# A two-layer kernel on one core: four reorderings around a saturated TensorE

## The reference, cut to what matters

```
# layer 0, x is (4, 512, 512) float32, V = 512, H = 2048
q, k, v = x @ Wq, x @ Wk, x @ Wv
attn_out = softmax(q k^T * V**-0.5) @ v @ Wp + bp
cms_out  = gelu(attn_out @ cW1 + cb1) @ cW2 + cb2 + one_hot(codes)
modifier = gelu(concat[attn_out, cms_out] @ mW1 + mb1) @ mW2 + mb2
x = clip(x + cms_out + modifier, 0, 1)
# layer 1, the adapter: weights picked by stream
h = gelu(x @ W_down[stream] + b_down[stream]) @ W_up[stream] + b_up[stream]
out = layernorm(x + h) * ln_w[stream] + ln_b[stream]
```

## Time and profile before

| | |
|---|---|
| time, median of 3 runs | 1076.12 us (1076.08 to 1076.13) |
| profiled execution's own time | 1076.47 us |
| its span | 1074.7 us |
| PE busy | 1064.8 us, 99% of the span |
| PEld, DVE, POOL, ACT busy | 882.2, 595.4, 541.8, 455.7 us |

### The profile page before, as it was taken

The page is one execution under the profiler, slowest core; times in us unless marked ns, Lnnn a source line. Parts: engine busy times, 40 slices in busy tenths (PEclk is TensorE's granted clock), DMA queues, the critical chain, the costliest instruction groups (busy, mean ns, idle before and its releaser), DMA issues.

```text
span 1074.7 us, 13175 instructions
## 1 busy us (share of the span) xinstructions
PE 1064.8 (99%) x4756; PEld 882.2 (82%) x4756; DVE 595.4 (55%) x837; ACT 455.7 (42%) x871; POOL 541.8 (50%) x555
## 2 busy tenths in 40 slices
PE   9999999999999999999999999999999999999997
PEld 8888888888888888888878888888878888888886
DVE  3735344395565565565764445445885454545568
ACT  4624336353343343333454333343644433342675
POOL 0501154542243232332798667666997667753415
PEclk9999999999999999999999999999999999999999
DMA  7401010101223213102222222224935221124863
GB/s 275 138 1 40 1 40 20 40 0 45 74 73 127 95 73 105 39 34 65 71 96 84 84 84 66 82 84 146 355 108 171 84 79 57 62 69 148 293 118 118
DMA packets 62064, 100.51 MB, mean 94 GB/s; under 512 B 5680, under 2 KB 35376, under 8 KB 61488
## 3 DMA queue, kind: packets, MB, share of 16 engines
q1 hardware_dynamic: 61424, 98.62, 27.1%
q10 hardware_dynamic: 576, 1.05, 0.3%
HBM read 77.63 MB, written 22.02 MB: 93 GB/s over the span
## 4 chain that ended last, share of the span: by engine, by line
PE 90%; DVE 4%; POOL 4%; ACT 1%; issue 1%; DMA 0%; ACTq 0%; DVEq 0%; POOLq 0%
PE bank L735 29%; PE bank L736 29%; PE bank L737 29%; DVE z L1512 1%; POOL left_c L567 1%; DVE stats L1506 1%; PE bank L789 1%; DVE c_T_f L1311 1%; POOL c_B_lo L567 1%; POOL rawC L581 1%; POOL W_lo L567 0%; DVE acc L1388 0%; PE bank L761 0%; POOL left_x L567 0%; POOL c_T_lo L567 0%
## 5 line engine op out<-in xcount | busy, mean ns | idle before, releaser
L1388 DVE TENSOR_TENSOR acc<-bank,acc 128x512 f32<-128x512 f32 x224 | 151.5, 688 | 89.7 <-PE bank L737 89.1
L735 PE MATMUL bank<-H_hi,W_hi 128*128 128x512 f32 x512 | 199.5, 390 | 1.4 <-POOL W_lo L567 1.4
L736 PE MATMUL bank<-H_lo,W_hi 128*128 128x512 f32 x512 | 199.4, 390 | 0.0
L737 PE MATMUL bank<-H_hi,W_lo 128*128 128x512 f32 x512 | 199.4, 389 | 0.0
L567 POOL TENSOR_TENSOR left_x<-rawX,left_x 128x256 fp32r<-128x256 f32 x144 | 125.9, 875 | 99.6 <-ACT left_x L986 99.6
L986 ACT ACTIVATE left_x<-rawX 128x256 fp32r<-128x256 f32 x144 | 57.9, 410 | 164.6 <-DMA rawX<-mW_dram 77.9
L1371 DVE TENSOR_TENSOR u_t<-bank,s_t 128x512 f32<-128x512 f32 x64 | 44.2, 691 | 131.5 <-PE bank L737 126.9
L735 PEld LDWEIGHTS bank<-H_hi,W_hi 128*128 128x128 f32 x512 | 96.1, 188 | 21.8 <-POOL W_lo L567 1.8
L737 PEld LDWEIGHTS bank<-H_hi,W_lo 128*128 128x128 f32 x512 | 96.2, 188 | 19.9
L736 PEld LDWEIGHTS bank<-H_lo,W_hi 128*128 128x128 f32 x512 | 96.2, 188 | 19.8
L737 PE MATMUL bank<-x_T_hi,left_x 128*128 128x512 f32 x256 | 99.7, 389 | 0.0
(11 more groups left out here) (195 smaller groups left out, 2313.8 us busy)
## 6 DMA issues: line engine op xcount, KB each, us to landing
rawX<-mW_dram SPq DMA_DIRECT2D x16, 512.0 KB, 3.8
rawC<-mW_dram SPq DMA_DIRECT2D x16, 512.0 KB, 5.0
W_raw<-mW_dram SPq DMA_DIRECT2D x16, 512.0 KB, 3.6
xT_raw<-xT_dram SPq DMA_DIRECT2D x4, 1024.0 KB, 8.6
x_raw<-x_dram SPq DMA_DIRECT2D x4, 1024.0 KB, 6.1
rawX<-cW_dram SPq DMA_DIRECT2D x8, 512.0 KB, 3.7
W_raw<-cW_dram SPq DMA_DIRECT2D x8, 512.0 KB, 3.7
out_dram<-z SPq DMA_DIRECT2D x16, 256.0 KB, 2.0
```

Of the source, the lines that this page charges most:

```text
L735: pe.matmul(tile, sh, mh, start=first_one and n == 0, stop=False, skip_group_check=joined_group)
L736: pe.matmul(tile, sh, ml, start=False, stop=False, skip_group_check=joined_group)
L737: last = pe.matmul(tile, sl, mh, start=False, stop=last_one and n == len(terms) - 1, skip_group_check=joined_group)
L1388: op = dve.tensor_tensor(dst, src, dst, ALU.add)
```

## The change

Four places are reordered. In the head, DVE instead of ACT rounds the first slice of WkT, WARM goes from 20 to 17, and the k = 0 matmuls with WqT_lo go ahead of those with WkT_lo. In group 16 POOL does the c sums ahead of `second_lo`. In group 24 ACT does `second_hi` ahead of the gelu of C21. In the tail PE does down(3) ahead of up(0), and ACT and DVE do the gelu of batch 3 ahead of all norms.

```diff
+        WkT0_hi_made = sem("WkT0_hi_made")
-        WARM = 20
+        WARM = 17
...
                     sum_2(*sets[0])
                     for i in (1, 2):
                         left_lo(*sets[0], i)
+                    sums_13(*sets[1])
+                    left_lo(*sets[1], 0)
+                    sum_2(*sets[1])
                     second_lo(second_set(g))
-                    left_lo(*sets[1], 0)
-                    sums_13(*sets[1])
-                    sum_2(*sets[1])
                     left_lo(*sets[1], 1)
...
-            pe.wait_ge(WqkT_hi_made, 2)
+            pe.wait_ge(WkT0_hi_made, 1)
+            pe.wait_ge(WqkT_hi_made, 1)
             for m in range(KT):
                 pe.matmul(bank_of(m)[:, :], WqT_hi[:, 0, cols(m)], WkT_hi[:, 0, :], start=True, stop=False)
+            pe.wait_ge(WqkT_lo_made, 1)
+            for m in range(KT):
+                pe.matmul(bank_of(m)[:, :], WqT_lo[:, 0, cols(m)], WkT_hi[:, 0, :], start=False, stop=False)
             pe.wait_ge(WqkT_lo_made, 2)
             for m in range(KT):
                 pe.matmul(bank_of(m)[:, :], WqT_hi[:, 0, cols(m)], WkT_lo[:, 0, :], start=False, stop=False)
-                pe.matmul(bank_of(m)[:, :], WqT_lo[:, 0, cols(m)], WkT_hi[:, 0, :], start=False, stop=False)
...
             adapter_down(2)
+            adapter_down(3)
             adapter_up(0)
-            adapter_down(3)
             adapter_up(1)
...
                 act.activation(WqT_hi[:, k, :], WqT_raw[:, k, :], ACT.Copy).then_inc(WqkT_hi_made, 1)
+                if k == 0:
+                    continue
...
                 if g == 23:
                     co_hi(1, T2)
+                if g in (23, 24):
                     second_hi(second_set(g))
                 gelu(g, C21)
...
-                if g > MOD0 and g != 23:
+                if g > MOD0 and g not in (23, 24):
                     second_hi(second_set(g))
...
             gelu_adapter(2)
-            for t in range(TT):
-                norm(t)
+            gelu_adapter(3)
             add_b_up(3)
-            gelu_adapter(3)
-            for n in range(TT, TT * B):
+            for n in range(TT * B):
                 norm(n)
...
+            dve.wait_ge(WkT_loaded[0], 16)
+            dve.tensor_copy(WkT_hi[:, 0, :], WkT_raw[:, 0, :]).then_inc(WkT0_hi_made, 1)
...
             gelu_lo_adapter(2)
+            gelu_lo_adapter(3)
             layer_norm(0)
-            gelu_lo_adapter(3)
             layer_norm(1)
```

More of the change, by code:

```diff
@@ L1238, in attn_f @@
                     dve.tensor_scalar(ops[op][2][:, k, :], bank_of(n)[:, :], column, None, ALU.add).then_inc(lo_made, 1)
+            dve.wait_ge(WkT_loaded[0], 16)
+            dve.tensor_copy(WkT_hi[:, 0, :], WkT_raw[:, 0, :]).then_inc(WkT0_hi_made, 1)
             for k in range(KT):
-                dve.wait_ge(WqkT_hi_made, 2 * k + 1)
+                dve.wait_ge(WqkT_hi_made, max(2 * k, 1))
                 dve.tensor_tensor(WqT_lo[:, k, :], WqT_raw[:, k, :], f32(WqT_hi[:, k, :]), ALU.subtract).then_inc(WqkT_lo_made, 1)
-                dve.wait_ge(WqkT_hi_made, 2 * k + 2)
+                if k == 0:
+                    dve.wait_ge(WkT0_hi_made, 1)
+                else:
+                    dve.wait_ge(WqkT_hi_made, 2 * k + 1)
                 dve.tensor_tensor(WkT_lo[:, k, :], WkT_raw[:, k, :], f32(WkT_hi[:, k, :]), ALU.subtract).then_inc(WqkT_lo_made, 1)
```

## The result

The changed kernel takes 1074.22 us (median of 20 runs, 1073.55 to 1074.81), the kernel before in the same comparison 1076.36 (20 runs, 1076.08 to 1077.25). The ratio is 0.9979, with a 95% interval of 0.9972 to 0.9985: 2.14 us, or 0.2%, faster. Forecast were 1073.95 and 2.17 less. The comparison leaves runs out in which the chip was disturbed. The profiled execution took 1073.88, its span is 1072.0 us; before it was 1076.47 and 1074.7.

What follows compares the result with a forecast made beforehand. TensorE was taken as the bound, busy 1064.8 of 1074.7 us. Gains of 0.33 + 0.72 + 0.57 + 0.55 = 2.17 us from the median of 1076.12 gave 1073.95 us, 8-in-10 range 1073.2 to 1075.0.

Steps and rivals of the forecast that it cites:

- The ceiling and the places: Whole kernel: only 9.9 us of the span are not TensorE's; gains only in head, two PE waits and tail, shifts additive.
- all later work has slack: Behind the head: with no PE waits other than two (1.4 and 0.7 us), early shifts stay to the end.
- The head: Program start: first matmul 0.5 us earlier, partly spent at half pace; gain 0.33 us, bounds 0 and 0.55.
- this moment is fixed: Head: TensorE's pace doubles at about 6.0 us, before and after the change; the three times before lay within 0.05 us.
- Group 16: PE's wait for left_c: POOL's 0.59 us idle goes, 0.2 to 0.3 of bubble stays; gain 0.72, bounds 0.1 and 1.0.
- the rival of the closing bubbles: Groups 16 and 24: PE finds operands nearly in time, 0.3 and up to 0.5 us more gain, 1073.2 us; chance 0.16.
- POOL's own work until left_lo(c, 1) stays the same: Group 16: reordering leaves POOL's work unchanged, so 0.59 us of idle goes, and about 0.1 between dependent sums.
- The feared wait for rawC: Group 16: POOL's earlier sums need rawC, with a margin of 0.1 us; each microsecond late costs PE one.
- Group 24: PE's wait for W_lo: H_lo and W_lo queue one after the other; gain 0.57 us, or 1.1 if they overlap.
- The tail: After the last matmul: DVE catches up by row 15, barely; gain 0.55 us, bounds 0.3 and 0.56.
- The port: Groups 16 and 24: one more DVE operation (0.6 us) before left_lo(c, 1), a clip (0.3) before W_lo; 1074.8 us; chance 0.16.
- the half pace behind a gap: Head: a gap after 17 transposes delays the rise, matmuls stay 0.44 us apart, kernel slower; chance 0.03.

Runs made afterwards that it cites:

- e2: The kernel before with only GpSimd's new order in group 16: 1075.58 us, ratio 0.9990.
- e3: The kernel before with only ScalarE's new order in group 24 (W_hi rounded before the gelu of C21): 1075.72 us, ratio 0.9992.
- e4: The kernel before with only the tail's new order on PE, ACT and DVE: 1075.73 us, ratio 0.9992.
- e5: The kernel before, unchanged, timed and profiled a second time: 1076.44 us, beside 1076.62 for the kernel before in that comparison.
- e1: The kernel before with only the head's part (DVE rounds the first WkT slice, 17 transposes, WqT_lo products first): 1076.93 us, ratio 1.0001.
- e10: The changed kernel with GpSimd's W_lo of group 24 moved ahead of sum_4 and both left_lo of product 4: 1073.75 us, ratio 0.9977 to the kernel before.
- e6: The changed kernel, unchanged, timed and profiled a second time: 1074.29 us, ratio 0.9978 to the kernel before.
- e8: The changed kernel with 12 warm-up transposes in place of 17: 1075.98 us, ratio 0.9991 to the kernel before.
- e12: The changed kernel with add_b_up(3) ahead of batch 3's gelu and group 24's W_lo ahead of sum_4: 1073.45 us, ratio 0.9972 to the kernel before.

## Why the prediction was right

The number was right: 1073.95 forecast and 1074.22 measured, 2.17 less and 2.14 less. By its own steps:

**The ceiling and the places.** The list of PE's waits carried the whole argument. All of the gain came from the four places, and nothing new held PE in the changed kernel. The shifts behind the head add within 0.05 us (e2, e3 and the whole). But the premise that all later work has slack as long as PE doesn't wait is too strong: in e4 a store that came late relative to PE (0.48 of waiting for 0.20) took back 0.32.

**The head**: 0.33 forecast. The mechanism was right, and so was about its size: the transposes end as the operands come (5.17 for 5.13), the new time is spent at half pace as long as the rise comes later, and at one moment of the rise the gain is 0.2 to 0.4. Wrong was the premise that this moment is fixed. I took three times within 0.05 us as evidence that it doesn't vary; in eleven runs of the same kernel (e5) the times lie 0.5 apart, and the rise came between 4.2 and 7.5 us. The 0.52 of the first pair of profiles is about 0.4 of change and 0.1 of luck. And the head has a cost that no row of before shows, the pause on DVE (0.46 for 0.10); in e1's profile it is what takes the head's gain back.

**Group 16**: 0.72 forecast, 1.03 measured, the bubble gone. This is the term that was mis-sized, and the rival of the closing bubbles had it: "0.3 more in group 16". What failed is the step that POOL's own work until left_lo(c, 1) stays the same. In before, left_lo(c, 0) takes 1.18 there, and the three sums behind it are long too:

```profile
554.80 1.24 POOL L602 TENSOR_TENSOR rawC_S<-rawC 128x256 f32<-128x256 f32 x1
556.00 1.23 POOL L581 TENSOR_TENSOR rawC<-rawC 128x256 f32<-128x256 f32 x1
557.32 1.06 POOL L581 TENSOR_TENSOR rawC<-rawC_S,rawC 128x256 f32<-128x256 f32 x1
```

In after each of these sums takes 0.74, and three operations are longer than alone: left_lo(c, 0) with 1.20, W_lo with 2.86 for 2.40, left_lo(c, 1) with 1.19 for 0.72. So four operations of POOL were held up beside DVE's in the old order and three are in the new. The six operations took 559.69 - 551.30 = 8.39 before and 558.04 - 550.79 = 7.25 now: 1.14 less, where the forecast had 0.59 and 0.1. The rest, 0.45, is about the one hold-up fewer (1.24 - 0.74 = 0.50). The feared wait for rawC did not come: the sums start at 550.79 with no idle time.

**Group 24**: 0.57 forecast, 0.64 and 0.63 measured. H_lo before W_lo, W_lo 2.88 where 2.9 was given, PE's wait 0.75 where 0.8 was given. Had I taken the overlap, it would have been 1.1. What remained was W_lo's place in POOL's list, which e10 changed.

**The tail**: 0.55 forecast, 0.56 alone (e4), 0.42 in the whole. The working was right, as e4 shows, which comes to the tail within 0.1 us of before. Row 1's statistics stand behind the first square root, at 1044.74 for the forecast 1044.7:

```profile
1044.66 0.17 DVE L1513 RECIPROCAL rstd<-std 128x1 f32<-128x1 f32 x1 [1.68 <-ACT std L1203]
1044.74 0.68 DVE L1504 BATCH_NORM_STATS2 stats<-bank 128x6 f32<-128x512 f32 x1
```

In the whole change they start at 1042.42, 2.32 earlier, and so does PE (last matmul at 1065.79 for 1068.11). DVE has caught up by row 15 with 1066.22 - 1066.00 = 0.22 to spare, "barely" as forecast; the pause of row 4 costs 0.36, so it used this up and 0.14 more. That pause is the cost that the forecast lacked.

**The sum** of what the runs bear out is 0.3 + 1.0 + 0.6 + 0.4 = 2.3 us, against 2.14 in the first comparison and 2.15 between the medians of e5 and e6 (2.33 between e6 and the kernel before beside it). Two terms were off by 0.3 and 0.1 in opposite directions, so that the total came within 0.03 of the forecast is luck. The result lies on the bound of 0.2% around which the forecast had split its chances.

**The rivals.** The port did not fall the other way; the bubbles closed in group 16, not in group 24; the half pace behind a gap exists (e8), but no trace with 17 transposes has such a gap.

## What to carry to other kernels

In a kernel that is 99% TensorE, cost a reordering at each wait of PE and split the result at starts that both traces have; the sum of the stretches then says which step was wrong, even when the total is right. Before a profile pair is read to a tenth of a microsecond, profile both kernels twice: here the start alone moves by one microsecond in the same program. And when a bubble is closed, a chain with a spread of its own can be the next to hold TensorE (the 1 MB store and load of e12), so look at the slowest runs and not only at the median.

## What was not expected of the hardware

- The moment at which TensorE's pace doubles at the start of the program was 4.2 to 7.5 us in thirteen traces, and beyond 9.4 with a gap of 0.7 ahead of the first matmul (e8), while the granted clock of these windows was given as full in all of them.
- One more copy and one more wait in DVE's program came with a pause of 0.46 us in place of 0.10 a thousand microseconds later, always ahead of the same instruction, in nine traces of nine.
- A VectorE operation held up by GpSimd's W_lo (2.41 long) took 2.46 in place of 0.68, and ended 0.55 after W_lo's row, so a little less than its own length (e10, and 2.29 in after).
- One load of 1 MB landed 5.4, 5.8 and 7.7 us after its issue in e10, after and e12.
